# Layer 1 of a graph network: window sums with the one-hot as the stationary operand, copied and turned a step later

## The reference, cut to what matters

```python
# layer 0
msg = relu(x[src] + (edge_attr @ W_edge + b_edge))
agg = segment_sum(msg, dst)                     # per destination node
h = relu((x + agg) @ W1 + b1) @ W2 + b2
x = layernorm(x + relu(batchnorm(h)))
# layer 1: attention with 4 heads of 64
z  = x @ W                                      # 6250 x 256
e  = leaky_relu(es[src] + ed[dst]);  e = where(e == 0, -1000, e)
ex = exp(e - segment_max(e, dst)[dst])
out = segment_sum(ex * z[src], dst) / segment_sum(ex, dst)   # per head
x = layernorm(x + out)
```

## Time and profile before

| | |
|---|---|
| median of 3 runs | 5301.25 us |
| the profiled execution | 5306.98 us, its span 5305.1 us |
| granted TensorE clock, mean | 0.833 of full speed |
| TensorE busy (products) | 3940.2 us, 74% |
| weight loads | 2743.8 us, 52% |
| VectorE busy | 2240.2 us, 42% |
| ScalarE busy | 718.8 us, 14% |
| GpSimd busy | 3028.8 us, 57% |
| DMA | 650 MB, mean 123 GB/s |
| layer 0's gathers | from 13 us to about 2500 us |
| layer 1's gathers | from 2617 us to 5266 us |

### The profile page before, as it was taken

The page is one execution under the profiler, slowest core; times in us unless marked ns, Lnnn a source line. Parts: engine busy times, 40 slices in busy tenths (PEclk is TensorE's granted clock), DMA queues, the critical chain, the costliest instruction groups (busy, mean ns, idle before and its releaser), DMA issues.

```text
span 5305.1 us, 63952 instructions
## 1 busy us (share of the span) xinstructions
PE 3940.2 (74%) x19180; PEld 2743.8 (52%) x19281; DVE 2240.2 (42%) x4481; ACT 718.8 (14%) x1302; POOL 3028.8 (57%) x3229
## 2 busy tenths in 40 slices
PE   6777777778877777777677777776776777777776
PEld 4555555556655555555544444444444444444444
DVE  4333333233332332323544445544555455555555
ACT  2121111112221221112400000000000001001001
POOL 6666656566655555555455555555655555555553
PEclk9888888888888888888877877887877887877777
DMA  4444444344443443433544444444443444443432
GB/s 147 130 132 132 129 126 130 119 131 133 125 129 118 131 128 115 123 115 101 143 122 117 121 120 123 125 120 119 125 119 116 120 124 125 120 123 111 118 114 81
DMA packets 321270, 650.08 MB, mean 123 GB/s; under 512 B 149823, under 2 KB 170537, under 8 KB 321225
## 3 DMA queue, kind: packets, MB, share of 16 engines
q0 software_dynamic: 150272, 413.00, 27.0%
q1 hardware_dynamic: 164681, 230.37, 13.9%
q10 hardware_dynamic: 6272, 6.19, 0.4%
HBM read 636.22 MB, written 13.08 MB: 122 GB/s over the span
## 4 chain that ended last, share of the span: by engine, by line
PE 39%; another core or an unknown queue 24%; issue 18%; DVEq 9%; DVE 8%; ACT 1%; DMA 0%; ACTq 0%; SPq 0%; POOLq 0%
PE psum L685 14%; PE psum L998 7%; PE psum L687 7%; PE psum L1009 5%; DVEq L1152 3%; DVE rows L1136 2%; PE psum L995 1%; DVEq L821 1%; DVE hot_t L854 1%; DVE rows L933 1%; DVEq L863 1%; PE psum L1037 1%; DVEq L1147 1%; DVEq L859 1%
## 5 line engine op out<-in xcount | busy, mean ns | idle before, releaser
L407 POOL DMA_INDIRECT rows<-z_tab,idx x1568 | 1500.3, 957 | 1150.0 <-issue 452.7
L407 POOL DMA_INDIRECT rows<-in_x,idx x1568 | 1491.4, 951 | 1012.4 <-issue 454.2
L685 PE MATMUL psum<-onehot,rows 128*128 128x128 f32 x6272 | 1345.2, 340 | 379.6 <-issue 374.8
L685 PEld LDWEIGHTS psum<-onehot,rows 128*128 128x128 f32 x6272 | 992.9, 223 | 792.1 <-issue 787.5
L1136 DVE TENSOR_TENSOR rows<-rows,psum 128x1024 f32<-128x1024 f32 x392 | 475.6, 1221 | 1706.1 <-remote 1065.9
L998 PE MATMUL psum<-weights,edge_room 128*128 128x256 f32 x3136 | 899.5, 411 | 120.5 <-issue 84.7
L1009 PE MATMUL psum<-rows,onehot 128*128 128x256 f32 x3136 | 860.1, 411 | 130.6 <-issue 126.0
L687 PE MATMUL psum<-onehot,rows 128*4 128x128 f32 x3136 | 687.2, 303 | 129.3 <-issue 128.5
L998 PEld LDWEIGHTS psum<-weights,edge_room 128*128 128x128 f32 x3136 | 658.0, 210 | 233.5 <-issue 78.8
L1009 PEld LDWEIGHTS psum<-rows,onehot 128*128 128x128 f32 x3136 | 627.9, 207 | 263.4 <-issue 184.5
L1082 ACT ACTIVATE rows<-rows 128x1024 f32<-128x1024 f32 x392 | 414.3, 1057 | 1981.3 <-DVE rows L1136 1565.6
(11 more groups left out here) (152 smaller groups left out, 1461.5 us busy)
## 6 DMA issues: line engine op xcount, KB each, us to landing
dst_t<-in_dst_jp SPq DMA_DIRECT2D x197, 512.0 KB
edge_room<-in_edge_t SPq DMA_DIRECT2D x196, 512.0 KB
rows<-in_x,idx POOLq DMA_INDIRECT x1568
rows<-z_tab,idx POOLq DMA_INDIRECT x1568
z_tab<-edge_room SPq DMA_DIRECT2D x14, 455.0 KB, 6.5
idx<-in_src_idx SPq DMA_DIRECT2D x392, 4.0 KB
dst_t<-in_x_t SPq DMA_DIRECT2D x14, 448.0 KB
rows<-in_x_t SPq DMA_DIRECT2D x14, 448.0 KB, 5.1
```

The costliest lines, as they stand in the source:

```text
L407: nc.gpsimd.indirect_dma_start(rows[0:count, u, j, 0:width], None, table, bass.IndirectOffsetOnAxis(ap=idx[0:count, u, j:j + 1], axis=0)). ...
L685: pe.matmul(banks[first + k][:, 0:WIN], rows[:, u, j, k * P:(k + 1) * P], hot, start=(j == 0), stop=(j == J - 1))
```

## The change

Layer 1's sum takes layer 0's form. The one-hot is stationary, the rows with their 4 exponentials move (260 columns), 8 products per group, into bank 4 or 5 by the group's parity. ScalarE copies the bank to `agg_sb` behind the next group's exponentials (`copy_lagged`). TensorE turns the copy with three transposes into bank 3 at the head of its next body but one, so turn of g - 2, sum of g - 1, small products of g + 1 (`turn_lagged`, `sum_lagged`). VectorE adds it two groups late instead of one. GpSimd waits for `agg_ready` (the sum is in its bank) in place of `turned`; VectorE waits for it before it overwrites a one-hot. The lag in `node_ends` becomes 2; ScalarE's chunk end asks for one group less, and TensorE's wait for `group_done` at a chunk end is dropped, as later waits cover it.

```diff
@@ pass_gathers
-                    pool.wait_ge(L.turned if layer == 1 and begun else L.group_done, g - RING + 1)
+                    pool.wait_ge(L.agg_ready if layer == 1 and begun else L.group_done, g - RING + 1)
@@ pass_matmuls
                 def finish_nodes(c, done):
-                    pe.wait_ge(L.group_done, done)
                     x_part(c)
                     rest(c)
@@
-            def sum_turned(u, g, early):
-
-                first, den_bank = 6 - 2 * (u % 2), 3 - u % 2
+            def sum_lagged(u, g, early):
+
                 pe.wait_ge(L.onehot_ready, g + 1)
                 if not early:
-                    pe.wait_ge(L.group_done, g - 1)
+                    pe.wait_ge(L.agg_copied, g - 1)
                 for j in range(J):
                     if j % (J // msgs) == 0:
                         pe.wait_ge(L.msg_ready, msgs * g + j // (J // msgs) + 1)
-                    hot = onehot[:, u % 2, j, :]
-                    for k in range(HALF):
-                        pe.matmul(banks[first + k][:, 0:WIN], rows[:, u, j, k * P:(k + 1) * P], hot,
-                                  start=(j == 0), stop=(j == J - 1))
-                    last = pe.matmul(banks[den_bank][0:HEADS, 0:WIN], rows[:, u, j, D:ROW], hot,
+                    last = pe.matmul(banks[4 + u % 2][0:WIN, 0:width], onehot[:, u % 2, j, :], rows[:, u, j, 0:width],
                                      start=(j == 0), stop=(j == J - 1))
-                last.then_inc(L.turned, 1)
+                last.then_inc(L.agg_ready, 1)
+
+            def turn_lagged(g, early):
+                pe.wait_ge(L.agg_copied, g + 1)
+                if not early:
+                    pe.wait_ge(L.group_done, g)
+                pe.sem_inc(passed, 1)
+                for k in range(HALF):
+                    pe.transpose(banks[3][:, k * WIN:(k + 1) * WIN], agg_sb[:, k * P:(k + 1) * P], ident[:, :])
+                pe.transpose(banks[3][0:HEADS, HALF * WIN:(HALF + 1) * WIN], agg_sb[:, D:ROW],
+                             ident[:, :]).then_inc(L.turned, 1)
@@
                 if fast:
+                    if n >= 2:
+                        turn_lagged(g - 2, n == 2)
                     if n >= 1:
-                        sum_turned((u - 1) % RING, g - 1, n < 3)
+                        sum_lagged((u - 1) % RING, g - 1, n < 3)
                     spread_ed(i, u + 1, g + 1)
                     return
@@
             if layer == 1:
-                pe.wait_ge(L.group_done, GROUPS - 1)
                 x_part(c0 if fast else 0)
             if fast:
-                sum_turned(RING - 1, GROUPS - 1, False)
+                turn_lagged(GROUPS - 2, False)
+                sum_lagged(RING - 1, GROUPS - 1, False)
+                turn_lagged(GROUPS - 1, False)
@@ pass_act
+            def copy_lagged(u, g):
+                act.wait_ge(L.agg_ready, g + 1)
+                act.copy(agg_sb[:, 0:width], banks[4 + u % 2][0:WIN, 0:width]).then_inc(L.agg_copied, 1)
@@
-                    if not start and not fast:
+                    if not start and fast:
+                        copy_lagged((u - 1) % RING, g - 1)
+                    elif not start:
                         copy_first(g - 1, first_round(i) and g == 1)
@@
-                    rest(c, done)
+                    rest(c, done if isinstance(done, int) else done - 1)
@@ pass_vector
-            def add_turned(u, base):
-                first, den_bank = 6 - 2 * (u % 2), 3 - u % 2
+            def add_turned(base):
                 at = bass.ds(base, WIN)
-                dve.tensor_tensor(acc[:, :, at], acc[:, :, at], psum[:, first:first + 2, 0:WIN], ALU.add)
-                dve.tensor_tensor(den[:, at], den[:, at], banks[den_bank][0:HEADS, 0:WIN], ALU.add)
+                dve.tensor_tensor(acc[:, :, at], acc[:, :, at],
+                                  banks[3][:, 0:HALF * WIN].rearrange("p (k n) -> p k n", k=HALF), ALU.add)
+                dve.tensor_tensor(den[:, at], den[:, at], banks[3][0:HEADS, HALF * WIN:(HALF + 1) * WIN], ALU.add)
@@
                 if fast:
+                    if not (first_round(i) and g < 2):
+                        dve.wait_ge(L.agg_ready, g - 1)
                     make_onehot_psum(u % 2, offsets(g))
@@
-                if not (first_round(i) and g == 0):
-                    finish((u - 1) % RING, g - 1)
+                back = 1 + fast
+                if not (first_round(i) and g < back):
+                    finish((u - back) % RING, g - back)
@@
+            if fast:
+                finish(RING - 2, GROUPS - 2)
             finish(RING - 1, GROUPS - 1)
@@ block.vector
-            for n, lag in enumerate((LAG, 1)):
+            for n, lag in enumerate((LAG, 2)):
```

More of the change, by code:

```diff
@@ L803, in pass_act @@
                 x_part(c0 if fast else 0)
-            if not fast:
+            if fast:
+                copy_lagged(RING - 1, GROUPS - 1)
+            else:
                 copy_first(GROUPS - 1, False)
@@ L861, in finish @@
                     dve.wait_ge(L.turned, g + 1)
-                    add_turned(u, base)
+                    add_turned(base)
                     dve.drain().then_inc(L.group_done, 1)
```

## The result

The kernel after takes **4999.96 us** (median of 4 runs, 4977.87 to 5022.99), the kernel before beside it 5302.74 (4 runs, 5294.39 to 5315.04): a ratio of 0.9428, 95% interval 0.9379 to 0.9477. The forecast was 5166 with a range of 4950 to 5340. The sign was right and the time lies in the range, but the gain of 303 us is more than twice the forecast 136, near the rival "two bodies per double" (4950).

What follows compares the result with a forecast made beforehand. GpSimd's gathers in layer 1 were taken to be held by signals that come through when it pauses; -130 for shorter cycles and -5 at the end gave 5306.98 - 135 = 5172 profiled, so 5166 us, range 4950 to 5340.

Steps and rivals of the forecast that it cites:

- two bodies per double: Rival, 15%: VectorE finishes two bodies per two-group cycle of layer 1, 22.5 us a cycle, 11.25 a group; 4950 us.
- 671 us: Layer 1's GpSimd waits beyond its gathers' own pace; by TensorE throughput all would go, which the prediction did not believe.
- the floor: GpSimd's least time for layer 1's gathers, 1568 x 1.262 = 1979 us; a rival at 6% expected 4695 us.
- single cycle of 12.46 us: Layer 1: one group, then a GpSimd pause, 3508.11 to 3520.57; claimed to stay whatever the sum takes.
- the forecast's 2527: Layer 1's gather stretch: 183 groups at 12.46 us and 13 chunk ends at 19, against 2650, so -123.
- Layer 0 as a measure: Layer 0's idle of 0.647 us a gather applied to layer 1's 1568 gathers: 1014 us against 1150, -136.
- Chunk ends: Layer 1's 13 chunk ends that hold GpSimd 9.23 us stay, at 19 us each; change cost 0, bounds -20 to +20.
- The end: After layer 1's last messages, two sums of 7.7 us become two of 3.5 with turn and copy: about 5 us less.
- The copy: Added ScalarE copy in layer 1, 0.353 us as in layer 0, expected covered; without cover 70 us.
- The clock: TensorE's granted clock expected lower; sums at half clock, 8.4 us a group, cost only if ending after the congested stretch.
- Doubles everywhere: Slower rival, 20%: every layer 1 pause follows two groups; 0 to +165 us, 5380 in the middle.
- no double that costs 28: Layer 1: the shorter sum is through when the congested stretch ends, so no two-group cycle takes 28 us; taken as -130.

Runs made afterwards that it cites:

- a_quarter_3: Kernel after with layer 1's dst_t transfers cut to 256 of 1024 columns from the second round on: 5049.11 us beside 5298.76, ratio 0.9538.
- b_quarter_3: Kernel before with layer 1's dst_t transfers cut to 256 of 1024 columns from the second round on: 5297.92 us beside 5298.76, ratio 0.9997.
- a_more_pe_3: Kernel after with each product of layer 1's sum done twice, the second into an unused bank: 5171.41 us beside 5302.34, ratio 0.9809.
- the free pair: Kernels before and after, both unchanged, on an occasion when signals were not delayed: kernel after 4085.72 us beside 4089.13, ratio 0.9991.
- a_pace: Kernel after with a one-column memset behind every layer 1 gather and one GpSimd drain per group: 5160.55 us, ratio 0.9746.
- a_drain_pairs: Kernel after with a GpSimd drain before the gathers of every second group of layer 1: 4417.47 us beside 4094.36, ratio 1.0784.

## Why the prediction was right in sign and wrong in size

- **What bounds the kernel.** Right: GpSimd's pauses, not TensorE's throughput, and signals that come through when GpSimd stops. Right that 671 us would not go at once. Wrong: "a dst_t transfer issued inside a run of gathers starts a congested stretch". Most of it lies 7 us or more into a run of gathers, with a quarter of `dst_t`'s bytes as with all (a_quarter_3, b_quarter_3), and it is there in only one of two conditions. In the other TensorE's long sum is covered and GpSimd stands at the floor. As the same programs run there without any crawl, TensorE's instruction count alone does not make it.
- **The step that failed**: "`dst_t` is issued at that same hot_t, so the sum's signal still falls into the congested stretch ... the single cycle of 12.46 us stays, whatever the sum takes". The sum that decides starts at the head of the body, together with GpSimd. At 7.2 us it misses, at 6.1 it passes (a_more_pe_3 against the kernel after), and 83 of the kernel after's sums ended at 3.6 to 6.5 us and passed. Instead of 183 groups at 12.46 there are 166 in doubles and 14 in singles, 11.96 a group on average. Of the 142 us between the forecast's 2527 and the measured 2385 this is 183 x 0.50 = 92.
- **Layer 0 as a measure** gave 1014 us of idle; layer 1 came to 890.3, as its lag of two and 3.5 us of sum leave it better placed than layer 0's (984.8 in this run).
- **Chunk ends** were put at 19 us each, 13 of them. That term, with the other 3 of the 16 groups that are not in the 180, makes the other 50 us of the 142: forecast 13 x 19 + 3 x 12.46 = 284; measured 11 long singles of 16.02, the first four groups in 46.0 and the last in 10, 232. The wait that was 9.23 us has such a like now:

```profile
3290.83 0.95 POOL L407 DMA_INDIRECT rows<-z_tab,idx  x1 [5.48 <-PE psum L681]
```

- **The end**: 5 us forecast, 4.8 measured. **The copy**: 0.353 forecast, and it is covered:

```profile
L770 ACT COPY agg_sb<-psum 128x260 f32<-128x260 f32 x196 | 73.4, 375 | 1285.1 <-remote 993.1 <-PE psum L681 180.6 <-issue 111.5
```

- **The clock** fell, to 0.72 in a pair (row below): the granted clock was 0.65 over the first sum of the pair shown, and 1.00 over the second. The rule that the prediction took from the Trainium skill, "TensorE: Matmul & The Clock Gate", section "HAM oscillation — how this bites in real kernels", that short bursts between waits throttle the engine again, agrees with the fall, though not for every sum. It cost nothing that shows: the sum at 0.65 still ended after 6.1 us, and in the free pair the kernel after took as long as the one before at a mean clock of 0.889 against 0.950.

```profile
3109.00:3132.60 23.60, 10.81 (x56) 8.57 (x54) 12.87 (x33) 1.39 (x6) 15.30 (x17) 0.72 0.50 146
```

- **The rival "two bodies per double"** named the right mechanism at a 15% chance; its pause was taken as 2.3 us and is 3.8. By its own sum that is 0.75 us a group, 183 x 0.75 = 137, and puts its 4950 at some 5090; that 5000 was measured comes with the chunk ends and first groups (about 50) and layer 0 (31). "Doubles everywhere" was slower only from a pause of 6.1 us; it was right that doubles would be everywhere and wrong on their price. The forecast's -130 for "no double that costs 28" is close to what the lag alone gives (131 and 162 singles of 12.33 in a_more_pe_3): it priced half of the change.

## What to carry to other kernels

When several engines go on in the same instant, long after the row that they waited for has ended, look at what another engine had just stopped doing, and measure from its start and its end; a transfer issued nearby may only be what makes the stretch visible. Where signals stop passing at some point in a run of work, the length of what must signal before counts in a step: a sum made some 3.5 us shorter was worth nothing in one condition and half the gain in the other. And take the kernel before on more than one occasion: a gain of 5.7% here was a gain of 0.1% (0.9991) where the chip was free.

## What the runs showed of the hardware that I had not expected

- The same kernel took 4090 us on some occasions and 5300 on others, with the same gathers (0.955 us each), and both layers paid (GpSimd idle in layer 0 of the kernel before: 487 against 1012 us).
- Held-back, a wait whose signal was long raised ends up to 12 us late and on all engines at once, while the same kind of wait met a few us earlier ends at once (3433.84 to 3445.76, and 3429.09 to 3429.12). Transfers are not slower on the whole: the gathers' packets took about the same time of the DMA engines (29.0% of 5006 us, 35.0% of 4083).
- A drain on GpSimd leaves 2.76 us of idle behind eight gathers (a_pace, held-back) and 3.86 behind sixteen (a_drain_pairs, free); a memset of one column (0.12 us) between two gathers costs nothing (a_pace).
